# Attention stage: a later unit's inputs issued ahead of the next unit's mask rows and moves

## The reference, cut to what matters

```
full    = one_hot(top-2 of softmax(q @ Wgate)) * w, the shared ones 1/S; normalised -> rw
mask    = (rw != 0)
qe, ke  = q @ Wq_exp[h], k @ Wk_exp[h], one 64-wide block per memory r
qe, ke, ve = qe * mask, ke * mask, ve * mask
attn    = softmax(qe @ ke^T / 8)          # per sequence, head and memory
o       = sum over r of rw * (attn @ ve)
out     = (o * silu(g)) @ Wo
```

## Time and profile before

| | |
|---|---|
| median of 3 runs | 2963.82 us (2961.93 to 2968.57) |
| profiled execution | 2963.52 us, span 2961.8 us, mean granted clock 0.914 |
| busy, share of the span | PE 85%, DVE 60%, ACT 42%, POOL 33% |
| attention | from about 366 to 1172 us of the span |
| DMA over the span | 441.60 MB, mean 149 GB/s |
| SyncE's queue (q1) | 389.36 MB, 43.3% of 16 engines' span |

### The profile page before, as it was taken

The page is one execution under the profiler, slowest core; times in us unless marked ns, Lnnn a source line. Parts: engine busy times, 40 slices in busy tenths (PEclk is TensorE's granted clock), DMA queues, the critical chain, the costliest instruction groups (busy, mean ns, idle before and its releaser), DMA issues. The chain is left out here.

```text
span 2961.8 us, 32540 instructions
## 1 busy us (share of the span) xinstructions
PE 2509.6 (85%) x9340; PEld 1655.3 (56%) x9340; DVE 1791.9 (60%) x2651; ACT 1235.1 (42%) x2450; POOL 965.2 (33%) x1004
## 2 busy tenths in 40 slices
PE   7999859999999998793799999267998865699989
PEld 5778724444444444570688888143454424588867
DVE  4310228989989998553455554448999996411143
ACT  3222027777777776231455554362233213311121
POOL 0102023333333331546100000317999994101010
PEclk9999969999999997886899999578999998899979
DMA  5253356565665661855677663634444445200031
GB/s 178 81 179 113 99 123 155 156 158 152 154 155 156 160 157 58 254 212 208 242 230 230 229 229 132 193 114 163 158 171 168 172 164 164 78 29 21 0 107 64
DMA packets 298210, 441.60 MB, mean 149 GB/s; under 512 B 41592, under 2 KB 124552, under 8 KB 298096
## 3 DMA queue, kind: packets, MB, share of 16 engines
q1 hardware_dynamic: 263392, 389.36, 43.3%
q10 hardware_dynamic: 28720, 33.10, 3.2%
q0 software_dynamic: 5984, 17.73, 1.8%
HBM read 303.85 MB, written 94.32 MB: 134 GB/s over the span
## 5 line engine op out<-in xcount | busy, mean ns | idle before, releaser
L1000 ACT ACTIVATE attn_probs<-attn_ps_score,attn_nmax 128x512 f32<-128x512 f32 x512 | 343.0, 673 | 5.6 <-DVE attn_nmax L1076 4.5
L2463 PE MATMUL scan_ps_o<-scan_qs,scan_sel 128*128 128x512 f32 x512 | 263.6, 631 | 80.5 <-DVE scan_qs L2407 53.4
L913 PE MATMUL attn_ps_score<-attn_KK,attn_S 128*128 128x512 f32 x512 | 278.8, 545 | 51.9 <-ACT attn_probs L1000 48.9
L2425 DVE TENSOR_TENSOR_SCAN scan_st<-scan_ps_dec,scan_kv 128x512 f32<-128x512 f32 x256 | 306.2, 1211 | 18.0 <-POOL scan_kv L2377 17.6
L913 PEld LDWEIGHTS attn_ps_score<-attn_KK,attn_S 128*128 128x128 f32 x512 | 101.2, 198 | 225.1 <-ACT attn_probs L1000 195.1
L841 POOL TENSOR_TENSOR attn_masked<-attn_spread,attn_q 128x512 f32<-128x512 f32 x96 | 122.7, 1281 | 294.9 <-DMA attn_spread<-rows 189.3
L2463 PEld LDWEIGHTS scan_ps_o<-scan_qs,scan_sel 128*128 128x128 f32 x512 | 88.7, 193 | 231.2 <-DVE scan_qs L2407 144.8
L1090 DVE SCALAR_TENSOR_TENSOR attn_mixed<-attn_probs,attn_cf,attn_mixed 128x512 f32<-128x512 f32 x256 | 197.2, 770 | 9.0
L1065 DVE TENSOR_REDUCE attn_raw<-attn_ps_score 128x2 f32<-128x1024 f32 x128 | 155.9, 1218 | 32.2 <-PE attn_ps_score L915 31.7
L1010 ACT ACTIVATE attn_probs<-attn_probs,attn_cf 128x512 f32<-128x512 f32 x128 | 92.4, 722 | 194.1 <-DVE attn_cf L1081 194.1
L2377 POOL TENSOR_TENSOR scan_kv<-scan_vb,gla_gk 128x512 f32<-128x512 f32 x128 | 161.2, 1277 | 19.6 <-DMA scan_vb<-gv 9.4
(11 more groups left out here) (434 smaller groups left out, 6391.3 us busy)
## 6 DMA issues: line engine op xcount, KB each, us to landing
scan_vb<-gv SPq DMA_DIRECT2D x256, 256.0 KB
moe_raw<-in_L_ffn_gating SPq DMA_DIRECT2D x92, 512.0 KB, 4.6
attn_spread<-rows SPq DMA_DIRECT2D x64, 384.0 KB, 8.8
moe_raw<-in_L_ffn_linear SPq DMA_DIRECT2D x46, 512.0 KB, 4.4
attn_S<-attn_X SPq DMA_DIRECT2D x64, 256.0 KB, 4.3
attn_S<-attn_Y SPq DMA_DIRECT2D x128, 128.0 KB, 4.3
rows_x<-out_zeros SPq DMA_DIRECT2D x23, 512.0 KB, 9.1
moe_xb<-rows_x SPq DMA_DIRECT2D x23, 512.0 KB, 5.9
```

The lines of the kernel that those rows point to most:

```text
L913: nc.tensor.matmul(ps_score[n][:, j, :], S[p][:, 2 * n + j, cols], KK[p][:, :], start=True, stop=False)
L1000: nc.scalar.activation(probs[b][:, at_j, :], ps_score[n][:, j, :], ACT.Exp, bias=nmax[b][:, at_j:at_j + 1], accum_out=Z[b][:, at_j:at_j + ...
L2425: V.tensor_tensor_scan(st[r][:, :], ps_dec[n % 2][:, :], kv[r][:, :], 0.0, ALU.mult, ALU.add).then_inc(st_ready, 1)
L2463: nc.tensor.matmul(ps_o[w][:, :], sel[:, P - GPH - GPH * d:2 * P - GPH - GPH * d], qs[i % RING][:, :], start=(d == 0), stop=(d == HALF - 1 ...
```

## The change

In SyncE's `step`, the call of `inputs` for unit u+3 is put ahead of `mask_rows` and the two calls of `move` for unit u+1. Nothing else changes: the same DMAs, waits, buffers and semaphores, and the same code on the other engines. The order of step u becomes: inputs of unit u+3, mask rows and moves of unit u+1, keys of unit u+2, store of unit u-2, v and sg of unit u. The inputs' own wait, `exp_done >= 2u + 4`, now comes ahead of the mask rows' wait, `qk_done >= 8u`.

```diff
             def step(i, p, u, first):
+                if left(u) >= 3:
+                    inputs(1 - p, u + 3, False)
                 if left(u) >= 1:
                     mask_rows(1 - p, u + 1, first and p == 0)
                     move(1 - p, u + 1, AB)
                     move(1 - p, u + 1, SHARED)
-                if left(u) >= 3:
-                    inputs(1 - p, u + 3, False)
                 if left(u) >= 2:
                     keys(p, u + 2, False)
```

## The result

The change makes the kernel slower: 3001.23 us median (2985.97 to 3007.03, 4 runs) against 2964.38 us (4 runs) of the kernel before beside it, a ratio of 1.0116 with a 95% interval of 1.009 to 1.0142. The same file measured again in two later sessions gave 1.0069 (1.0041 to 1.0097) and 1.0133 (1.0078 to 1.0187). The forecast was 2959 us, the measured time lies 30 us above the upper end of the range.

The account below looks back on a forecast made before the run. The prediction took two DMA engines, loaded with q and k and never idle, to bound the stage. Zero for earlier issue and 4.5 us for the place in the queue: 2963.5 - 4.5 = 2959.0 us, range 2947 to 2971 us.

Parts of the forecast that it names:

- two DMA engines without free time: In the stage, two of 16 engines carry q and k, 0.459 MB a step each, and set 23.64 us a step.
- windows at 0.13: One-microsecond windows with SyncE held up at DMA share 0.13, two of 16 engines working; expected to remain after the change.
- VectorE's price: VectorE's wait for GpSimd's sums behind the late product, 1.16 us a step; expected to stay near 30 us over the stage.
- products over 23.8 us apart: Sign of crowding: GpSimd's products released by the spread rows spaced wider than 23.8 us, against 23.64 before.
- the 31.3 us: Rival that the whole wait goes: VectorE's 31.3 us of waiting vanish, giving 2932 us; chance 0.10.
- The single gain at the start: Inputs pass rows and moves on the two engines: spread rows land 4.5 us earlier, gained once, not 27 times.
- the queue's period stays 23.64 us, because its work is the same: On the DMA queue, the reordering leaves each step's time at 23.64 us.
- It is kept at the end: The 4.5 us survive to the stage's end, since the steps after the last inputs (unit 31) carry no inputs.
- the crowding grows: Rival: new neighbours slow the two engines' packets, 0.4 us a step, 10.8 us, 2970 us; decides from 0.17; chance 0.15.
- the loss of 4.9 us a step: Two engines' step of 23.64 us against 18.7 at quiet rate; the rest lost while the other fourteen are busy.
- The cycle's content is the same and only rotated: Argument against the rival that crowding grows by 8%, 10.8 us: each step issues the same DMAs; rival's chance 0.15.
- the moves as the next late thing: Moves of unit u+1 land later, leaving 5.4 us before TensorE's score matmul needs them; caps the gain at 5.4 us.

Follow-up runs that it names:

- two pairs: Moves, or spread DMAs, cut to 8 of 512 columns, q loaded twice; orders before and after: 1.0332 and 1.0129 (moves), 1.0151 and 1.0229 (spread).
- e5: Kernel after the change, with the two spread DMAs ahead of q and Wx inside inputs: 1.0034 of the time before, median 2977.88 us.

## Why the prediction was wrong

What bounds the stage, two DMA engines without free time, was right: taking q's extra load off them removes 2.5% of the time, and with q and k spread the order is without effect. (That load is 56 of some 213 to 216 packets of 2 KB a step, an estimate: 64 of q and 64 of k on each of the two, and a sixteenth of the other 1410 that the trace has in a step.) Much of the forecast view followed from it: the wait for the spread rows stays, SyncE's wait for the scores goes, the long issue appears behind q, windows at 0.13 remain. VectorE's price did not stay near 30 us: it went from 1.2 to 2.1 us a step. And the sign that the prediction itself had named for crowding, products over 23.8 us apart, came true. Whoever had booked the 31.3 us would have been wrong by twice their size.

The single gain at the start came: 4.5 us forecast, unit 1 starts 6.4 us earlier (7.7 and 6.8 in the repeats), of which 2.2 us (3.8 and 3.4) come from the stage's first unit starting earlier. That the sizes are close is partly luck. The forecast let compute run ahead by 1.16 us a step and reach 4.5 us after about four steps; the gain stands at unit 1 already, so this is not that mechanism at work. And it is not kept, because of the next step.

The step that failed is this one: "the queue's period stays 23.64 us, because its work is the same", and with it "The gain is paid once" and "It is kept at the end". The work in bytes is the same; the work in time is not. 24.79 - 23.64 = 1.15 us a step, over 27 steps 31 us, and that swallows the gain. I had named the cause as the rival "the crowding grows", with a deciding point of 0.17 us a step, and given it 0.15. What I sized wrong was its bound: I let the loss of 4.9 us a step grow by 8%, with no row for the 8%; it grew by 23%. The rows had the wider bound in them: 280 and 199 GB/s in two full windows, at an equal share. If the moves, 1.31 MB, go at 209 instead of 280 GB/s, all 16 engines are full for 6.3 instead of 4.7 us, 1.6 us longer, and the two engines with them. That is an estimate from single windows; the packet records give 1.1 us more a step with 14 or more packets under way, and as much more with just two. "The cycle's content is the same and only rotated" was the wrong argument against it: the rotation changed which transfers are under way together. My reading is that q, now directly ahead of the moves, leaves the two engines in arrears when the moves are offered to all 16, and both compete; no run shows this by itself.

How far the runs carry this: shown clear of noise are that q and Wx ahead cost (1.0063) where the spread rows alone don't (1.0017), that the loss stays whatever the moves read (HBM, 1.0100 against 1.0016), and that it goes when q is spread over all engines. That it takes the moves' bytes rests on two pairs of which one isn't clean and the other overlaps, and k ahead (1.0096) has SyncE's wait as a rival. The order spread rows, then q (e5) should lose the most by this reading, and its 1.0034 is less than that of q alone ahead. Why this overlap costs more than that of before, where the two engines carry the store, v and sg beside the moves, is not shown: the packets' records don't say which engine carried them.

The forecast of the moves as the next late thing did not come to be tested: among TensorE's waits after the change, 450 to 1150 us, none is put down to attn_S, and with steps of 24.79 us compute did not come nearer to the moves in the way that the forecast feared.

## What to carry to other kernels

If a load is late although its issue is early, look at what the DMA engines do while it is late: a share of 2/16 with SyncE held in an issue meant here that two engines bind, and then an earlier place in the program order left the wait where it was and made the pace worse. Look at transfers whose outer dimension is small, and spread them over all 16 engines before tuning the order; here that was worth 2.5%, and it made the two orders equal. On a bound queue, bound the price of a reordering by the slowest and the fastest full window of the trace and not by bytes: the same mix of bytes took 7% longer a packet.

## What the runs showed of the hardware that I had not expected

A packet costs by its company, at the same mix of sizes: 94.2 ns on average before, 101.2 after. Windows with a share of 0.95 or more carry 229 GB/s on average before and 208 after, and single ones from 199 to 280.

SyncE's issue of the DMA right behind q or k took 3.6 us (Wx after) to 6.2 us (the store before) when the two engines were in arrears, and 0.39 us (the store) with q and k by halves. Behind q in the step of the earlier trace rows Wx took 0.37 us, so such a transfer in front isn't enough by itself.

With q and k by halves the steps are 1.8 us shorter and TensorE's granted clock is 1.00 instead of 0.94. The gain of 76 us is more than twice the stall that the profile of before had put on the path (31.3 us); some 49 us of it lie in the steps and 21.5 us at the head of the stage, which the row of the stall did not cover. How much of the 49 us is the clock was not separated from the stalls.
